# Striking scores with a bf16 matmul in PSUM, and moving three side steps between engines

## What is computed

```python
q = (x @ Wq.T).reshape(b, n, 2, HEADS, DIM_KEY).transpose(2, 0, 1, 3, 4)
sim = jnp.einsum('pbnhd,hkpd->pbnhk', q, keys)
sx, ix = jax.lax.top_k(sim[0], TOPK)
sy, iy = jax.lax.top_k(sim[1], TOPK)
all_scores = (sx[..., :, None] + sy[..., None, :]).reshape(b, n, HEADS, TOPK * TOPK)
scores, pk_indices = jax.lax.top_k(all_scores, TOPK)
h = jax.nn.gelu(jnp.einsum('bnd,bnhkd->bnhk', x, W_down[pk_indices]), approximate=False)
h = h * jax.nn.softmax(scores, axis=-1)
return jnp.einsum('bnhk,bnhkd->bnd', h, W_up[pk_indices])
```

## Time and profile before

| | us |
|---|---|
| median of 3 runs | 278.73 |
| lowest and highest | 277.35, 278.85 |
| the profiled execution, its own time | 277.19 |
| its span, first to last instruction | 275.4 |
| outside the span | 1.8 |

### The profile page before, as it was taken

The page is one execution under the profiler, slowest core; times in us unless marked ns, Lnnn a source line. Parts: engine busy times, 40 slices in busy tenths (PEclk is TensorE's granted clock), DMA queues, the critical chain, the costliest instruction groups (busy, mean ns, idle before and its releaser), DMA issues.

```text
span 275.4 us, 7038 instructions
## 1 busy us (share of the span) xinstructions
PE 237.8 (86%) x1562; PEld 176.2 (64%) x1562; DVE 261.0 (95%) x1715; ACT 234.9 (85%) x1048; POOL 225.9 (82%) x344
## 2 busy tenths in 40 slices
PE   7799689897989988988898889988998899898891
PEld 7456343685668666765676577657765776587780
DVE  5899999999999999999999999999999999998985
ACT  2553866989899999999989999999999999998953
POOL 7889701467588979998999889988998899889972
PEclk9999999999899999999999999999999999999997
DMA  7930000000000000100000000100010001000102
GB/s 179 281 80 1 2 0 0 2 1 0 5 0 0 5 0 1 38 6 0 2 12 31 1 0 2 42 0 5 0 39 4 1 0 40 2 1 4 38 4 76
DMA packets 11228, 6.23 MB, mean 23 GB/s; under 512 B 1457, under 2 KB 10674, under 8 KB 11186
## 3 DMA queue, kind: packets, MB, share of 16 engines
q1 hardware_dynamic: 9858, 5.12, 7.0%
q10 hardware_dynamic: 1328, 0.66, 1.1%
HBM read 3.67 MB, written 2.10 MB: 21 GB/s over the span
## 4 chain that ended last, share of the span: by engine, by line
POOL 29%; PE 29%; ACT 22%; issue 14%; DVE 5%; POOLq 0%; ACTq 0%; DVEq 0%
POOL past L487 4%; PE scratch L1662 4%; PE sim L1570 4%; POOL squareT L502 4%; ACT prob L847 3%; POOL drop L509 3%; POOL wgt L515 3%; PE s_bank L1764 3%; PE s_bank L1758 2%; ACT gap L769 2%; ACT spare L866 2%; PE t_bank L1588 2%; PE s_bank L1553 2%; POOL wgt L523 2%; ACT side L739 2%
## 5 line engine op out<-in xcount | busy, mean ns | idle before, releaser
L1215 DVE MAX8 top<-rest 128x8 f32<-128x40 f32 x512 | 57.4, 191 | 0.1
L1165 DVE MAX8 top<-sim 128x8 f32<-128x32 f32 x496 | 54.0, 184 | 0.0
L847 ACT ACTIVATE prob<-drop 128x50 f32<-128x50 f32 x224 | 51.5, 254 | 0.0
L847 ACT ACTIVATION_READ_ACCUMULATOR prob<-drop 128x1 f32 x224 | 46.9, 211 | 0.0
L502 POOL TENSOR_TENSOR squareT<-sideT 100x512 bf16<-100x512 bf16 x31 | 32.6, 1050 | 4.8 <-ACT sideT L757 4.8
L487 POOL TENSOR_TENSOR past<-gap,last 128x400 f32<-128x400 f32 x31 | 26.8, 864 | 9.5 <-DVE last L1239 9.5
L1570 PE MATMUL sim<-sim_w,xT_all 128*128 128x512 f32 x64 | 33.9, 611 | 0.5 <-ACT xT_all L794 0.5
L509 POOL TENSOR_TENSOR drop<-gap,out_by 128x400 f32<-128x400 f32 x30 | 31.0, 1033 | 1.2 <-ACT out_by L746 1.2
L1588 PE MATMUL t_bank<-gaps_of,topT 128*128 128x200 f32 x128 | 30.1, 359 | 2.0 <-ACT topT L762 2.0
L515 POOL TENSOR_TENSOR wgt<-prob,rden 128x400 f32<-128x400 f32 x30 | 25.7, 856 | 5.9 <-DVE rden L1157 5.9
L1239 DVE MAX8 last<-slot_gap 128x8 f32<-128x22 f32 x256 | 24.4, 169 | 1.1
(11 more groups left out here) (295 smaller groups left out, 755.7 us busy)
## 6 DMA issues: line engine op xcount, KB each, us to landing
out<-y_sb SPq DMA_DIRECT2D x7, 256.0 KB, 2.3
x_sb<-in_L_attn_hidden_states SPq DMA_DIRECT2D x2, 256.0 KB, 3.8
fwq_sb<-in_L_ffn_Wq ACTq DMA_DIRECT2D x2, 256.0 KB, 5.6
x_sb<-in_L_attn_hidden_states SPq DMA_DIRECT2D x1, 512.0 KB, 5.3
wc_sb<-in_L_attn_Wc SPq DMA_DIRECT2D x1, 256.0 KB
out<-last_y SPq DMA_DIRECT2D x2, 128.0 KB, 1.9
wo_in<-in_L_attn_Wo SPq DMA_DIRECT2D x1, 192.0 KB
keys_sb<-in_L_ffn_keys ACTq DMA_DIRECT2D x1, 128.0 KB, 3.3
```

The source lines that it names most:

```text
L847: last = nc.scalar.activation(prob[d][:, h, :], drop[:, h, :], ACT.Exp, scale=-1.0, accum_out=den[d][:, h:h + 1])
L1165: last = nc.vector.max(top[n % 3][:, v, 0:8], sim_bank[n % 2][:, bass.ts(v, KEYS)])
L1215: last = nc.vector.max(top[n % 3][:, v, 8:16], rest[:, v, :])
```

## The change

- `strike_above` runs on DVE only for tiles 0 to 3. For tiles 4 to 31 PE adds the strikes into the score bank with a bf16 matmul of `above` and -1e38 times the identity (`strike`, first in PE's turn), and ACT copies the struck scores into `rest` (`take_struck`, first in ACT's turn). `rest` has two buffers, and `scores(n + 2)` waits for the copy.
- Counts and tie slots leave the score bank for the new SBUF buffers `counts` and `tie`. In DVE's turn `spill_above` and `put_ties` move ahead.
- `past` is made in bf16 and transposed directly; `side_of` goes, and the sign is taken in `take_sides`. `last_past_of` reads the gaps from PSUM.
- For the tiles n from 3 to 28 with n % 4 equal to 0 or 3 (14 tiles) DVE makes `drop` from the counts in `f_bank` and `gap` in one instruction (`keep_gaps`); ACT's `out_by_of` and POOL's `drop_of` skip these tiles.

The core of the diff:

```diff
-        rest = sb("rest", [P, VECS, KEYS + 8])
+        rest = [sb(f"rest{i}", [P, VECS, KEYS + 8]) for i in range(2)]
+        strike16 = sb("strike16", [P, P], BF16)
+        counts = sb("counts", [P, VECS])
+        tie = sb("tie", [P, VECS, 8])
...
-        past = sb("past", [P, HEADS, CANDS])
-        side = sb("side", [P, HEADS, CANDS], BF16)
+        past = sb("past", [P, HEADS, CANDS], BF16)
...
+        def kept_by_vector(n):
+
+            return TB - 1 <= n < TILES - 3 and n % TB in (0, TB - 1)
...
             def drop_of(n):
 
-                pool.wait_ge(out_by_done, n + 1)
+                if kept_by_vector(n):
+                    return
+                pool.wait_ge(out_by_done, out_bys_until(n))
...
-                nc.scalar.activation(sideT[0:TWO, :], f_bank[0:TWO, :], ACT.Copy).then_inc(sideT_out, 1)
+                nc.scalar.activation(sideT[0:TWO, :], f_bank[0:TWO, :], ACT.Sign).then_inc(sideT_out, 1)
+
+            def take_struck(n):
+
+                act.wait_ge(struck, n - TB + 1)
+                act.wait_ge(top_done, 2 * n - 2)
+                nc.scalar.activation(rest[n % 2][:, :, 0:KEYS], sim_bank[n % 2][:, :].rearrange("p (v k) -> p v k", k=KEYS),
+                                     ACT.Copy).then_inc(sim_used, 1)
...
                 if n >= 1:
                     dve.wait_ge(summed_above, n)
+                    if n <= TB:
+                        dve.wait_ge(sim_used, n)
+                    else:
+                        dve.wait_ge(struck, n - TB)
                 nc.vector.tensor_tensor(above[:, :, :], sim_bank[n % 2][:, :].rearrange("p (v k) -> p v k", k=KEYS),
                                         eighth(n, KEYS), ALU.is_ge).then_inc(above_done, 1)
...
-                nc.vector.tensor_reduce(sim_bank[n % 2][:, 0:TIES], above[:, :, :], AX_X, ALU.add
-                                        ).then_inc(summed_above, 1)
...
+                nc.vector.tensor_reduce(counts[:, :], above[:, :, :], AX_X, ALU.add).then_inc(summed_above, 1)
...
-                nc.vector.scalar_tensor_tensor(tie_slots(n),
-                                               sim_bank[n % 2][:, 0:TIES].unsqueeze(2).to_broadcast([P, VECS, 8]), 2.0,
+                nc.vector.scalar_tensor_tensor(tie[:, :, :], counts[:, :].unsqueeze(2).to_broadcast([P, VECS, 8]), 2.0,
                                                rank_row[:, 7:15].unsqueeze(1).to_broadcast([P, VECS, 8]),
                                                ALU.mult, ALU.subtract).then_inc(spill_done, 1)
...
-                nc.vector.scalar_tensor_tensor(rest[:, :, KEYS:KEYS + 8], tie_slots(n), SPILL, eighth(n, 8),
-                                               ALU.mult, ALU.min).then_inc(sim_used, 1)
+                if n >= 1:
+                    dve.wait_ge(top_done, 2 * n)
+                nc.vector.scalar_tensor_tensor(rest[n % 2][:, :, KEYS:KEYS + 8], tie[:, :, :], SPILL, eighth(n, 8),
+                                               ALU.mult, ALU.min).then_inc(ties_done, 1)
...
+            def keep_gaps(n):
+
+                dve.wait_ge(count_ready, n + 1)
+                dve.wait_ge(gap_out, n + 1)
+                dve.wait_ge(prob_done, n)
+                nc.vector.scalar_tensor_tensor(drop[:, :, :].rearrange("p h c -> p (h c)"),
+                                               f_bank[:, 0:HEADS * CANDS], OUT_SCALE,
+                                               gap[n % 4][:, :, :].rearrange("p h c -> p (h c)"),
+                                               ALU.mult, ALU.max).then_inc(drop_done, 1)
...
                 b, j = divmod(n, TB)
-                strike_above(n)
+                sum_above(n)
                 if n + 1 in tiles:
                     first_8(n + 1, [0])
-                sum_above(n)
+                spill_above(n)
                 invert_sums(n - 4)
-                spill_above(n)
                 if j == 0:
                     maxima(b - 1)
+                put_ties(n)
+                if kept_by_vector(n - 3):
+                    keep_gaps(n - 3)
                 if n + 1 in tiles:
                     first_8(n + 1, [1])
-                put_ties(n)
-                if n + 1 in tiles:
                     mark_above(n + 1)
                 next_8(n, 0)
...
-                nc.vector.tensor_tensor(past[:, :, :], gap[m % 4][:, :, :],
+                nc.vector.tensor_tensor(past[:, :, :],
+                                        t_bank[:, 0:HEADS * CANDS].rearrange("p (h c) -> p h c", c=CANDS),
                                         last8[m % 2][:, :, 7:8].to_broadcast([P, HEADS, CANDS]),
...
+            def strike(n):
+
+                pe.wait_ge(above_done, n + 1)
+                mm(sim_bank[n % 2][:, :], strike16[:, :], above[:, :, :].rearrange("p v k -> p (v k)"),
+                   start=False, stop=True, skip_group_check=True).then_inc(struck, 1)
...
                 elif n >= 1:
-                    pe.wait_ge(out_by_done, n)
+                    pe.wait_ge(out_by_done, out_bys_until(n - 1))
```

More of the change, by code:

```diff
@@ L274, in program @@
         sim_ready, sim_top8, sim_used, top_done = sem("sim_ready"), sem("sim_top8"), sem("sim_used"), sem("top_done")
-        above_done, struck, summed_above, spill_done = (
-            sem(n) for n in ("above_done", "struck", "summed_above", "spill_done"))
+        above_done, struck, summed_above, spill_done, ties_done = (
+            sem(n) for n in ("above_done", "struck", "summed_above", "spill_done", "ties_done"))
         topT_ready, topT_out, gap_ready, gap_out = (sem(n) for n in ("topT_ready", "topT_out", "gap_ready", "gap_out"))
-        slot_gap_done, last8_done, past_done, side_done = (
-            sem(n) for n in ("slot_gap_done", "last8_done", "past_done", "side_done"))
+        slot_gap_done, last8_done, past_done = (sem(n) for n in ("slot_gap_done", "last8_done", "past_done"))
         ahead_done, count_q_done, count_full, count_in = (
@@ L336, in summed, with out_bys_until @@
             return n >= TILES - 4
+        def kept_by_vector(n):
+            return TB - 1 <= n < TILES - 3 and n % TB in (0, TB - 1)
+        def out_bys_until(n):
+            return sum(not kept_by_vector(m) for m in range(n + 1))
         def sums_until(n):
@@ L752, in take_sides @@
                 if n == TILES - 1:
-                    nc.scalar.activation(last_sideT[0:TWO, :], t_bank[0:TWO, :], ACT.Copy).then_inc(sideT_out, 1)
+                    nc.scalar.activation(last_sideT[0:TWO, :], t_bank[0:TWO, :], ACT.Sign).then_inc(sideT_out, 1)
                     return
@@ L819, in _ @@
             take_topT(1)
-            side_of(0)
             take_gaps(1)
@@ L917, in last_squares @@
             def last_squares():
-                nc.scalar.activation(last_squareT[0:TWO, :], t_bank[0:TWO, :], ACT.Square).then_inc(last_square, 1)
+                act.wait_ge(sideT_out, TILES)
+                nc.scalar.activation(last_squareT[0:TWO, :], last_sideT[0:TWO, :], ACT.Square).then_inc(last_square, 1)
             def late_tanh():
@@ L987, in turn @@
                 b, j = divmod(n, TB)
+                take_struck(n)
                 if j == 0:
@@ L1054, in _ @@
             take_sides(0)
-            side_of(1)
             unit(0, U_KW, [(kw[:, :], 0, bk_sb, 1.0)])
@@ L1592, in transpose_sides @@
             def transpose_sides(n):
-                pe.wait_ge(side_done, n + 1)
+                if n < TILES - 1:
+                    pe.wait_ge(past_done, n + 1)
+                else:
+                    pe.wait_ge(last_past, 1)
                 dst = f_bank if n < TILES - 1 else t_bank
@@ L1596, in transpose_sides @@
                     pe.wait_ge(slot_gap_done, 2 * TILES)
+                elif n >= 1 and kept_by_vector(n - 1):
+                    pe.wait_ge(drop_done, n)
                 elif n >= 1:
-                    pe.wait_ge(out_by_done, n)
+                    pe.wait_ge(out_by_done, out_bys_until(n - 1))
                 for k in range(HEADS // 2):
-                    last = mm(dst[0:TWO, bass.ts(k, P)], side[:, 2 * k:2 * k + 2, :].rearrange("p h c -> p (h c)"),
+                    last = mm(dst[0:TWO, bass.ts(k, P)], past[:, 2 * k:2 * k + 2, :].rearrange("p h c -> p (h c)"),
                               ident16[:, :], start=True, stop=True)
@@ L1772, in turn @@
                 b, j = divmod(n, TB)
+                strike(n)
                 if j == 0:
```

27 lines of the change are left out of this document (12 added, 15 removed).

## The result

The changed kernel takes **289.94 us** (median of 4 runs, 287.77 to 290.49) against 278.04 us of the kernel before (4 runs, 277.33 to 278.85). The ratio is 1.040, with a 95% interval of 1.036 to 1.044: slower by 4.0%, where 3.3% was forecast. The profiled execution takes 289.87 us: 12.7 us more than that of the kernel before, where the sum gave 9.2.

A forecast was written before the change was run, and what follows sets the result against it. DVE, busy 98% of the turns, was taken as the bound. Terms -16.5 + 6.7 + 19.6 + 0.5 - 1.1 = +9.2 us on 277.19 gave 286.4, for the median 288.0 us, range 273 to 297.

The forecast's parts named there:

- head +0.5: In the head, the ties of tiles 0 to 3 meet POOL's row norms: +0.5 us.
- Two of its signs: Expected in the trace after: DVE at 97% or more of the turns; tie instructions together about 0.7 us longer.
- W = 0.7 us a turn: In DVE's turns, spill_above and put_ties with SBUF inputs wait for POOL's current instruction: +19.6 us over 28 turns.
- rival 1: In the turns, DVE mostly asks while POOL waits for it, tie waits 0.1 us a turn: 271.1 us, chance 0.19.
- Its waits are old ones: In DVE's turns, keep_gaps waits only for exponentials that invert_sums needs anyway and counts from PE's turn before.
- "nothing" for PE: In the turns, PE's 28 added bf16 matmuls of 512 columns fit in 20 us of idle time: no cost.
- rival 3: Struck scores' round trip DVE, PE, ACT, DVE also binds; DVE stands before next_8: +7, 295 us, chance 0.1.
- The strikes, -16.5: In DVE's queue, the strike's 0.59 us goes in 28 turns: -16.5 us.
- ACT's relief: In the turns, ACT's queue gets a net 4.1 us lighter; not the bound, so nothing in the sum.
- `keep_gaps`, 0.48 us each: In DVE's queue, the added instruction costs 0.48 us in each of 14 tiles: +6.7 us.
- `rstd` left out of the lock: POOL's reciprocal square root was taken not to hold DVE; counting it would make the sum about 1 us larger.
- The second rule: scalar_tensor_tensor with two non-bf16 SBUF sources runs at half throughput: an estimated 7 us more, not put in the sum.

The follow-up runs named there:

- f_sides: The kernel before with only the signs' part: past in bf16, side_of gone, sign taken in take_sides, last past read from PSUM; 273.35 us.
- l_sides_ties_sbuf: `f_sides` plus counts and tie slots in SBUF instead of the score bank; 293.06 us.
- e_no_keep: The changed kernel with keep_gaps left out, so ACT and POOL make all kept gaps again; 280.87 us.
- a_ties_sbuf: The kernel before with only counts and tie slots moved from the score bank to SBUF, in the old order; 294.26 us.
- g_score_bank: The changed kernel with counts and tie slots back in the score bank, made by DVE after ACT's copy of the struck scores; 279.14 us.
- c_late_max: The changed kernel with maxima at j = 0 moved two steps later, behind the second first_8; 288.68 us.
- h_bank_no_keep: `g_score_bank` without keep_gaps, so all kept gaps are on ACT and POOL; 281.31 us.

## Why the prediction was right, and where it was not

The sign held, and so did its cause: the tie instructions wait for POOL once their operands lie in SBUF, and that costs more than the strikes' removal saves. The size came out near partly by luck. The runs give the parts as a chain of kernels that differ by one part each, from the kernel before (278.7 us in that run, 278.3 and 278.4 in two others) to the change:

| step | measured us | forecast us |
|---|---|---|
| signs alone: before to `f_sides` | -5.3 | -1.1 |
| ties in SBUF: to `l_sides_ties_sbuf` | +19.7 | +19.6 and head +0.5 |
| strikes on PE and ACT, new order: to `e_no_keep` | -12.2 | -16.5 |
| `keep_gaps`: to the change | +9.1 | +6.7 |

The steps come from different runs and each is good to 1 us or so. They add up to +11.3 where the forecast parts add up to +9.2. But the two largest misses, 4.2 us of gain overlooked in the signs and 4.3 us too much gain for the strikes, cancel each other, and nothing in the prediction made them do so. Two of its signs also failed in the trace after: DVE is busy 95% of the turns, not 97% or more, and the tie pair takes 0.5 us more than before, not 0.7.

- **The ties' waits, W = 0.7 us a turn.** The mechanism is shown: `a_ties_sbuf` loses 16 us by this alone, `l_sides_ties_sbuf` 19.7, and `g_score_bank` gets 10.8 us back. In the changed kernel the 56 instructions of the 28 turns lie 14.1 us above the free 0.27 to 0.29, W = 0.50. By j it is 0.2, 0.9, 0 and 0.9 for j = 0 to 3, forecast 0.75, 0.75, 0.2 and 1.1. Without `keep_gaps` W is 0.68 over the 28 turns. So the 0.7 fits the change without `keep_gaps`, which is not the kernel that it was worked out for, and that is chance: the working had `drop` gone from POOL at half of the tiles. (Its 0.3 us for a request at a random time is the price of one request; two a turn make 0.6.) The difference is `spill_above` at j = 0: it takes 1.24 to 1.27 us there, and 0.27 in the changed kernel, where it falls (150.36 to 150.63) into a time in which POOL stands:

```profile
150.95 1.03 POOL L520 TENSOR_TENSOR drop<-gap,out_by 128x400 f32<-128x400 f32 x1 [0.94 <-ACT out_by L749]
```

  At j = 2 rival 1's mechanism is seen (POOL waits for `rden` while DVE asks), in one turn of four and not in all. The ties of tiles 0 to 3 cost 0.7 us, forecast 0.5.
- **The step that failed: "Its waits are old ones", of `keep_gaps`, and "nothing" for PE.** I asked what DVE waits for in `keep_gaps`, and of those behind it I named PE's sides only in rival 3. The missed chain is: DVE comes to `maxima` 0.59 us earlier, since the strike is gone from its queue, and PE comes to its block scores later, since its transposes wait for `keep_gaps` (6.2 us in eight of them). The row at j = 0 is

```profile
151.48 0.49 DVE L1302 TENSOR_REDUCE nmax<-s_bank 128x4 f32<-128x320 f32 x1 [0.74 <-PE s_bank L1738]
```

  and PE's matmul L1738 there starts at 151.12 and takes 0.33. The wait is 7.1 us longer than before over the turns. Moving `maxima` alone gives nothing (`c_late_max`). Put into the sum it reads -16.5 + 6.7 + 14.1 + 0.5 + 7.1 - 1.1 = +10.8, against 12.7 of the profiled executions. With all of DVE's waits in the window (9.0 us after, 2.8 before) in place of this one it is +9.9, so 2 to 3 us have no place in the sum. The turns' end alone, the start of DVE's last pass of `next_8`, moved from 250.18 to 263.24.
- **The granted clock has a share that the prediction had not.** The seven waits for the block scores are 0.39, 0.74, 1.94, 0.74, 0.74, 1.47 and 1.71 us. Ahead of the three long ones the clock was granted at its lower level, 1.2 of 2.4 GHz, for about 3 us each (0.50 from 116 to 119 us). PE's `sim` matmuls L1590 take 1.89 us there, at 116.58, and 1.04 at full clock, at 147.00. The stretch ahead of the long wait at 122.26, and the same stretch two batch rows on, ahead of the 0.74 at 181.26, in the columns of the earlier trace rows:

```profile
114.00:121.00 7.00, 6.44 (x36) 5.30 (x37) 6.25 (x47) 5.11 (x26) 4.70 (x6) 0.76 0.14 42
...
172.00:179.00 7.00, 5.42 (x34) 4.33 (x34) 6.93 (x46) 4.72 (x26) 5.78 (x8) 1.00 0.01 1
```
```profile
122.26 0.49 DVE L1302 TENSOR_REDUCE nmax<-s_bank 128x4 f32<-128x320 f32 x1 [1.94 <-PE s_bank L1738]
```

  The three exceed 0.74 by 2.9 us together, so of the 7.1 us about 4 are the missed chain and about 3 went with the lower clock. The executions of the kernel before say the same: of the 38 within 1.5% of its fastest, the 13 with a mean granted clock of 0.994 or more have a median of 277.4 us, the 9 with 0.986 or less one of 279.3. The profiled executions have 0.988 before and 0.973 after, for which a line through the 38 gives an estimated 1.9 us. Where DVE doesn't wait for PE the clock matters less: the four executions of `l_sides_ties_sbuf`, with 0.927 to 0.980, lie within 1.4 us of one another. Before each of the three falls PE had stood 1.0 to 1.25 us waiting for `keep_gaps`; but it did so at 144.93 and 174.71 too, and the clock stayed. Whether the change itself brings the clock down is not shown.
- **The strikes, -16.5.** Their 0.59 us each is right only while DVE is what everyone waits for. Where the ties hold DVE, the edit gave 12.2 us. Where they don't, no gain showed: `h_bank_no_keep` is 8 us above `f_sides`, though it differs from it in the order of the ties too. That looks like rival 3, but rival 3's own sign is absent: in neither `h_bank_no_keep` nor the changed kernel does DVE stand ahead of `next_8`, so the struck copy was there in time. DVE waits for other work of ACT (`p_cs`, `prob`) and PE, whose queues the strikes had lengthened or moved.
- **ACT's relief "not binding", so nothing.** Mis-sized: the 2% of idle time that the earlier trace rows leave to DVE are 4 us of the 185, and in `f_sides` most of them came back. That is -5.3 instead of -1.1.
- **`keep_gaps`, 0.48 us each**: 7.2 us on top of `f_sides` against 6.7, with a share of the low clock in it, and its 0.56 us duration as in the earlier trace rows. The `past` of the tail fell from 1.62 to 0.57 us as forecast.
- **`rstd` left out of the lock.** The row that spoke for it comes again in the changed kernel's trace, where the 2-element `nmr` takes 0.15 us at 281.27 while POOL's `rstd` runs from 281.02 to 281.72. No tie instruction met a short `rstd` at a telling phase, so its share in the turns stays open. The second rule that the prediction takes from the Trainium skill (Vector Engine (DVE) Microarchitecture Reference, section "Points that are easy to get wrong"), halved throughput with two SBUF sources that are not bf16, does not show: beside an idle POOL the SBUF ties take 0.27 and 0.29 us, and with one input in PSUM they took 0.30 and 0.28.

## What to carry to other kernels

Before an operand of VectorE moves from PSUM to SBUF, look at what GpSimd does at that point of the loop: here two small instructions a turn cost more than the 512-element one whose removal brought them. Where one engine is 98% busy, what relieves its neighbours can give back its last 2%. What relieves the engine itself by sending its work over two engines that are nearly as full may give less than it took off: 12.2 of 16.5 us here, and no gain in the kernels whose ties lay in PSUM. A composite change wants each part run by itself on the kernel before: here one of four parts was worth 1.8% by itself, and the others hid it.

## What had not been expected of the hardware

- GpSimd's next instruction can come in ahead of a VectorE instruction that already stands. At 158.59 DVE asks while `past` (157.87, 0.86 us) has 0.14 us to go; POOL's `drop` follows it at 158.69, and DVE's 0.27 us come only behind that too: 1.28 us, its end at 159.87 against `drop`'s at 159.71.

```profile
157.87 0.86 POOL L496 TENSOR_TENSOR past<-gap,last 128x400 bf16<-128x400 f32 x1
```

  In `a_ties_sbuf` it is more: at 159.38 `drop` (158.93, 1.03 us) has 0.58 us to go, `weigh` follows it (159.91, 0.86 us), and DVE's instruction takes 1.54 us, to 160.92. So the price is not always what was left of one instruction. The Trainium skill, SBUF — State Buffer, section "SBUF: two separate sides", has the two engines lock each other out for whole instructions; the durations agree with that, and no run here shows by what rule the next holder is chosen.
- The phase of two engines that hold each other can repeat every four turns to 0.02 us: in `a_ties_sbuf` the j = 1 instructions L1203 take 1.55, 1.54, 1.54, 1.55, 1.54 and 1.53 us in six rows of the batch one after another. In the changed kernel it does not: there the j = 1 wait falls on `spill_above` in three rows of the batch and on `put_ties` in four.
